# Attention layers: seven batches in one block with counting semaphores, a deferred MLP residual, and constant rows filled by DMA

## The reference

```python
h = _modulate(_layernorm(x), shift_msa, scale_msa)
x = x + gate_msa * _attention(h, ...)            # softmax(q k^T / sqrt(d)) v, projected
h = _modulate(_layernorm(x), shift_mlp, scale_mlp)
x = x + gate_mlp * (gelu(h @ W1 + b1) @ W2 + b2)
```

## Time and profile before

| | us |
|---|---|
| median of 3 runs | 6445.23 |
| the profiled execution | 6451.02 |
| its span | 6449.2 |
| setup, to the start of layer 0's first batch | 91.6 |
| layer 0, eight batches | 915 |
| layer 1, eight batches | 1567 |
| layer 2, eight batches | 986 |
| layer 3, eight batches | 2890 |

### The profile page before, as it was taken

How to read it: one execution, slowest core, us unless ns; L and a number is a source line. 1 busy time by engine, 2 the same in 40 slices (tenths; PEclk the granted TensorE clock), 3 DMA queues, 4 the chain that set the end, 5 groups by cost and what they waited for, 6 DMA issues and landing times. The chain is left out here.

```text
span 6449.2 us, 77669 instructions
## 1 busy us (share of the span) xinstructions
PE 5852.0 (91%) x28624; PEld 3040.1 (47%) x28624; DVE 4487.7 (70%) x4943; ACT 4214.9 (65%) x6876; POOL 2663.0 (41%) x1964
## 2 busy tenths in 40 slices
PE   8899899999999998998998888988898888888887
PEld 4444444555554554444444444444444444444444
DVE  5665654334444345666565998989898998989897
ACT  2354445444455443443434998989898998989896
POOL 0000002222222222000000886959596886959596
PEclk8999999999999999999999999999999999999999
DMA  4313220000000002222131202010101102011100
GB/s 114 60 30 54 36 50 22 1 1 1 1 1 1 1 1 48 40 48 47 32 59 23 59 21 55 29 49 29 47 30 35 41 22 55 29 47 30 47 29 19
DMA packets 152665, 216.11 MB, mean 34 GB/s; under 512 B 24224, under 2 KB 91064, under 8 KB 152032
## 3 DMA queue, kind: packets, MB, share of 16 engines
q1 hardware_dynamic: 152288, 211.14, 14.3%
HBM read 146.54 MB, written 30.44 MB: 27 GB/s over the span
## 5 line engine op out<-in xcount | busy, mean ns | idle before, releaser
L2230 DVE TENSOR_TENSOR_SCAN l__h<-l__decay,psum 128x1024 f32<-128x1024 f32 x1024 | 2276.5, 2272 | 79.1 <-ACT l__decay L1826 28.4
L2214 POOL TENSOR_TENSOR l__hc<-l__h,l__c_rep 128x1024 f32<-128x1024 f32 x1024 | 2039.0, 2004 | 189.2 <-DVE l__h L2230 126.6
L1826 ACT ACTIVATE l__decay<-l__dt_rep,l__a_neg 128x511 f32<-128x511 f32 x2048 | 1485.5, 845 | 14.9 <-DVE l__h L2230 14.8
L1833 PEld LDWEIGHTS psum<-ident,l__dtx_B 128*128 128x128 f32 x8192 | 892.2, 142 | 1108.8 <-DVE l__h L2230 683.1
L1833 PE MATMUL psum<-ident,l__dtx_B 128*128 128x128 f32 x8192 | 1132.0, 282 | 264.0 <-ACT l__dtx_B L1811 186.9
L1811 ACT ACTIVATE l__dtx_B<-l__dtx_T,l__b_T 128x512 f32<-128x512 f32 x1792 | 1328.4, 839 | 37.8 <-PEq L2325 35.8
L2299 PE MATMUL psum<-l__hc,l__gather 128*64 128x512 f32 x4096 | 1116.6, 624 | 10.2 <-POOL l__hc L2214 9.7
L193 POOL TENSOR_SCALAR l__ln_var_eps<-l__ln_mean_var 128x4 f32<-128x4 f32 x64 | 17.9, 279 | 2103.3 <-DVE l__ln_mean_var L179 2102.7
L675 DVE TENSOR_REDUCE l__row_max<-psum 128x1 f32<-128x512 f32 x1024 | 659.1, 687 | 267.1 <-PE psum L690 265.4
L1335 POOL TENSOR_SCALAR l__probs<-l__probs,l__rec 128x512 f32<-128x512 f32 x512 | 351.1, 699 | 966.7 <-DVE l__rec L1331 966.6
L1007 ACT ACTIVATE l__probs<-psum 128x1024 f32<-128x1024 f32 x512 | 516.4, 1026 | 285.4 <-PE psum L1068 278.6
(11 more groups left out here) (165 smaller groups left out, 7069.8 us busy)
## 6 DMA issues: line engine op xcount, KB each, us to landing
l__c_rep<-l__c_dram SPq DMA_DIRECT2D x512, 128.0 KB, 2.8
l__dt_rep<-l__dt SPq DMA_DIRECT2D x128, 256.0 KB, 5.1
l__parts_dram<-l__parts SPq DMA_DIRECT2D x64, 384.0 KB, 3.6
l__q_stack<-l__parts_dram SPq DMA_DIRECT2D x192, 128.0 KB, 6.4
l__k_stack<-l__parts_dram SPq DMA_DIRECT2D x192, 128.0 KB, 8.8
l__w<-in_l_w SPq DMA_DIRECT2D x6, 1024.0 KB, 7.6
in_mod_w<-in_mod_w SPq DMA_DIRECT2D x1, 4608.0 KB, 16.4
out_x<-x_sb SPq DMA_DIRECT2D x8, 512.0 KB, 3.2
```

What stands on the lines that cost most here:

```text
L1826: nc.scalar.activation(decay[:, i % DECAYS, s, 1:T], dt_rep[:, w, c, s, 1:T], ACT.Exp, scale=a_neg[:, g, c, s:s + 1]).then_inc(S["decay"], 1)
L1833: last = nc.tensor.transpose(bx_psum(i)[:, s, t * P:(t + 1) * P], dtx_B[:, (k + 1) % 2, t, 2 * c + s, :, :].rearrange("p j d -> p (j d)"), ...
L2214: nc.gpsimd.tensor_tensor(hc[:, i % HCS, :, :], h[:, i % HS, :, :], c_of_i, ALU.mult).then_inc(S["hc"], 1)
L2230: nc.vector.tensor_tensor_scan(both(h[:, i % HS, :, :]), both(decay[:, i % DECAYS, :, :]), both(bx_psum(i)), 0.0, ALU.mult, ALU.add).then_ ...
```

## The change

- `Semaphores` gets a count for each batch (`each`) and `at(name, n)`, which gives the semaphore and `batch * each + n`; all waits go through it.
- In the narrow and the wide layers the engines' programs are functions of a batch (`sync_batch`, `gpsimd_batch`, `vector_batch`, `scalar_batch`, `tensor_batch`). Batches 0 to 6 are one block without barriers between them, batch 7 is a second block. Layer 3 keeps a block for each batch.
- Waits that were only implied by the barrier are written out: the first late scores on the early maxima, `scores_T(0)` on the first max rows, `values(0)` and the first max transposes on the residual, in the wide layer the first scores, transposes and projection on what the batch before still held.
- Narrow layers, batches 0 to 5: the MLP residual is done in the next batch, after its third late tile (`RESIDUAL_AT = LEAD + 2`); the `cur` copy and the gates' products move there too. The other batches keep it at their end.
- Narrow layers: the first max rows of the next batch are made after early tile 20 (`FIRST_ROWS_AT = GT + 4`) and not after tile 23.
- The constant rows of the key stack come by DMA from a row of ones in DRAM (`ones16`, written in the setup), no `memset`; `first_gpsimd` does not wait for `rstd` any more.
- Setup: `second_tensor` follows the 14th of the `REST` fills.

```diff
+    def at(self, name, n):
+        return self.of[name], self.batch * self.each.get(name, 0) + n
...
         def first_sync(sp):
             valid_sync(sp, 0)
-            qkv_sync(sp, 0, True)
+            for row in range(k_max, k_all):
+                sp.dma_start(ks[row:row + 1, :, :],
+                             io["ones16"].unsqueeze(1).broadcast_to([1, H, T])).then_inc(S["ones_in"], 16)
+            qkv_sync(sp, 0)
+            sp.wait_ge(*S.at("ones_in", 16 * (k_all - k_max)))
             max_rows_in(sp, 0, 1)
 
         def first_gpsimd(pool):
-            pool.wait_ge(S["rstd"], 1)
-            nc.gpsimd.memset(ks[STACK:k_all, :, :], 1.0).then_inc(S["ones"], 1)
-            pool.wait_ge(S["ones"], 1)
             nc.gpsimd.memset(va[:, :, :, HD:2 * HD], 1.0).then_inc(S["ones"], 1)
...
-                    second_tensor(pe)
                     rest = iter(setup.REST)
-                    for _ in range(len(setup.REST) - LEAD // 3):
+                    for n in range(len(setup.REST) - LEAD // 3):
                         setup.fill(pe, next(rest))
+                        if n == SECOND_AT:
+                            second_tensor(pe)
...
+            for n in range(LEAD, TILES + GT):
+                if n < TILES:
+                    take_max(dve, n, n - LEAD + 1)
+                if n == RESIDUAL_AT:
+                    if S.batch:
+                        S.batch -= 1
+                        mlp_residual(dve, x[:, b - 1, :, :])
+                        S.batch += 1
+                    nc.vector.tensor_copy(cur[:, :], mod[:, b, mod0:mod0 + n_mod]).then_inc(S["cur"], 1)
+                    if gated:
+                        dve.wait_ge(*S.at("cur", 1))
+                        gates.vector(nc, dve)
...
+                for n in range(LEAD):
+                    take_max(dve, n, LATER + n + 1)
+                    if n == FIRST_ROWS_AT:
+                        make_max_rows(dve, bank[EARLY_MAX_BANK], NG)
+            if b + 1 >= JOINED:
+                mlp_residual(dve, x_b)
...
+                        early_scores(pe, early, LATER)
+                        if early == FIRST_ROWS_AT:
+                            pe.wait_ge(*S.at("max_taken", LATER + GT))
+                            max_transposes(pe, 0, bank[EARLY_MAX_BANK])
+                        early += 1
...
         def body(following):
-            for b in range(B):
-                more, more2 = b + 1 < B, b + 2 < B
-                F = None if more else following
+            for part in (range(JOINED), range(JOINED, B)):
+                F = following if part.stop == B else None
                 with nc.Block() as block:
...
                     @block.tensor
                     def _(pe):
+                        for b in part:
+                            S.batch = b - part.start
+                            tensor_batch(pe, b, F)
...
                 m = 3 * pair + t
                 if t < 3 and m < IN_LOOP:
                     if m:
                         pe.wait_ge(*S.at("proj", m))
+                    elif S.batch:
+                        pe.wait_ge(*S.at("res", 1 - RES_STEPS))
                     project(pair_of(m), t, bank[PROJ_BANK])
```

More of the change, by code:

```diff
@@ L465, in mask_rows @@
     def mask_rows(self, dve):
+        self.nc.vector.memset(self.ones16[:, :], 1.0).then_inc(self.s_mask, 1)
         dve.wait_ge(self.s_mask_in, 16)
@@ L874, in alone, with about, mlp_residual, sync_batch @@
             nc.all_engine_barrier(sems_to_clear=S.range)
+        def about(b):
+            return b + 1 < B, b + 2 < B, x[:, b, :, :]
+        def mlp_residual(dve, x_b):
+            residual(nc, dve, S, bank[6:8], b2[:, :], gates.rows[:, 1, :] if gated else None, tmp, x_b, 1,
+                     "down_filled")
+        def sync_batch(sp, b, F):
+            more, more2, x_b = about(b)
+            if b == 0:
+                late_sync(sp)
+            if F:
+                F.load(sp)
+            if more:
+                valid_sync(sp, b + 1)
+            for gg in range(1, NG):
+                max_rows_in(sp, gg, gg)
+            if more:
+                qkv_sync(sp, b + 1)
+                max_rows_in(sp, 0, NG)
+            if F:
+                sp.wait_ge(*S.at("oT", NG))
+                F.sync(sp)
@@ new lines, in gpsimd_batch @@
+        def gpsimd_batch(pool, b, F):
+            more, more2, x_b = about(b)
+            if b == 0:
+                late_gpsimd(pool)
+            if F:
+                F.gpsimd_begin(pool)
+                F.rstd(pool)
+                pool.wait_ge(*S.at("oT", NG))
+                F.gpsimd_heads(pool)
+            norm.gpsimd(nc, pool, 0)
+            if more2:
+                norm.gpsimd(nc, pool, 1)
+            if F:
+                F.gpsimd(pool)
+                F.gpsimd_second(pool)
@@ L986, in _ @@
-                        if more2:
-                            ahead.vector(nc, dve, b + 2, 1)
-                        if more:
-                            for n in range(LEAD):
-                                take_max(dve, n, LATER + n + 1)
-                            make_max_rows(dve, bank[EARLY_MAX_BANK], NG)
-                        residual(nc, dve, S, bank[6:8], b2[:, :], gates.rows[:, 1, :] if gated else None, tmp, x_b, 1,
-                                 "down_filled")
-                        if F:
-                            F.vector_end(dve)
+                        for b in part:
+                            S.batch = b - part.start
+                            vector_batch(dve, b, F)
@@ new lines, in gpsimd_batch @@
+        def gpsimd_batch(pool, b, F):
+            more, n_mlp, x_b = about(b)
+            for i in range(EARLY):
+                if i == SCALED_AT - 1 and more:
+                    norm.gpsimd(nc, pool, 0)
+                if i == NEXT_SCALED_AT - 1 and F:
+                    F.rstd(pool)
+                pool.wait_ge(*S.at("rec", i + 1))
+                normalise(i + LEAD)
+            norm.gpsimd(nc, pool, n_mlp)
+            if more:
+                for i in range(EARLY, UNITS):
+                    pool.wait_ge(*S.at("rec", i + 1))
+                    normalise(i - EARLY)
+            if F:
+                pool.wait_ge(*S.at("oT", PAIRS))
+                pool.wait_ge(*S.at("rstd", n_mlp + 1))
+                F.gpsimd(pool)
+                F.gpsimd_second(pool)
@@ L1390, in body @@
+        def body(following):
+            for part in (range(JOINED), range(JOINED, B)):
+                F = following if part.stop == B else None
                 with nc.Block() as block:
@@ L1468, in _ @@
-                        if more:
-                            for i in range(EARLY, UNITS):
-                                maxima(i)
-                            for i in range(EARLY, UNITS):
-                                sums_inverted(i)
-                        residual(nc, dve, S, bank[6:8], b2[:, :], gates.rows[:, 1, :], tmp, x_b, 1, "down_filled")
+                        for b in part:
+                            S.batch = b - part.start
+                            vector_batch(dve, b, F)
```

1439 lines of the change are left out of this document (725 added, 714 removed).

## The result

| | before | after |
|---|---|---|
| median of four runs each, one chip, us | 6447.47 | 6409.89 (6409.23 to 6412.81) |
| ratio, 95% interval | | 0.9942 (0.993 to 0.9954) |
| span of the profiled execution, us | 6449.2 | 6408.5 |

The account below looks back on a forecast made before the run. TensorE, busy 91%, was taken as the bound, with idle time at barriers and holds. Layer 1 28.6, layer 0 13, layer 2 9, setup 9 and hand-over 7.5 sum to 67 us: 6445.2 to 6378 us, range 6348 to 6404.

Parts of the forecast that it names:

- Layer 1, 28.6 us: Wide layer, six barriers gone: TensorE's 3.44 us gaps close, 20.6 us, and cold clock starts vanish, 8 us.
- the hand-over, 7.5 us: Layer 1 to layer 2: without GpSimd's memset holding VectorE 6.4 us gained, plus 1.1 us less at 1.2 GHz.
- Setup, 9 us: Setup: earlier norm without the memset and fills put before the second transposes gain 9 us, bounds 5 and 10.
- The parts 2.6 and 6.4: Setup: norm 2.6 us earlier without the memset; TensorE's 6.75 us wait filled by 14 fills, less 0.4 us.
- the fills take the same in either clock (they are 8 columns wide): Setup: TensorE's fills were assumed to take 0.85 us each whatever the granted clock.
- Layers 0 and 2, 22 us: Narrow layers, six barriers gone each and residual deferred: 13 us in layer 0 and 9 us in layer 2.
- The count of VectorE's chain: Narrow-layer boundary, tiles 24 to 30: layer 0 has 10.9 us, 8.1 of it work; gain 2.5 us, layer 2 2.1.
- less 0.3 us since in such a pause the clock can fall too: Layer 0 boundary: clock allowance taken off the 2.5 us gain, leaving 2.2 us, six times.
- the 0.6 us of layer 2: Layer 2 boundary: allowance for the clock falling in the residual's pause, taken off 2.1 us, leaving 1.5 us.
- the residual eats the narrow layers' gain: Rival, chance 0.17: in the narrow layers' tile loop the residual makes TensorE idle and cool; 45 us saved, 6400 us.
- The other three: Rivals: whole pause absorbed (0.12, 6325 us); GpSimd's hold stays (0.06, 6387); late tiles stay at 1.2 GHz (0.03, 6571).
- narrow batches not shorter: Sign of being wrong: batches of layers 0 and 2 fail to shorten, against a forecast 1.5 to 2.5 us.

Follow-up runs that it names:

- experiment 7: The kernel after, with the key stack's ones written by GpSimd's memset again instead of by DMA: 6413.05 us, ratio 0.9962 to the kernel before.
- experiment 1: The kernel after, but narrow layers have a block and barrier per batch again, residual at its end, old tile order: 6395.23 us, ratio 0.9938 to the kernel before.
- experiment 12: The kernel after itself, unchanged, run again beside the other follow-ups: 6397.81 us, ratio 0.9945 to the kernel before.
- experiment 3: The kernel after without the MLP residual of batches 0 to 5 in both narrow layers (output incomplete): 6338.02 us, ratio 0.9848 to the kernel before.
- experiment 4: The kernel after, with ScalarE copying the MLP's banks to SBUF, VectorE adding the residual after the last tile's maximum, gates' copy later: 6322.47 us, ratio 0.9823.
- experiment 2: The kernel after, with the joined narrow batches' residual at the end of its own batch instead of after tile 26: 6399.22 us, ratio 0.9941.

## Why the prediction was wrong

- *Layer 1, 28.6 us, and the hand-over, 7.5 us*: right. The batches are 187.7 us as forecast, layer and hand-over together give 36.1 (29.4 and 6.7), and experiment 7 brings the hold back at 6.7 us.
- *Setup, 9 us*: 15.0 measured. The parts 2.6 and 6.4 are right (2.7 and 6.7). Wrong is "the fills take the same in either clock (they are 8 columns wide)": 0.45 us a fill at 2.4 GHz, 0.85 at 1.2, and eleven of the 28 run at 2.4 GHz now. 4.5 us. The last 1.1 us are not accounted for.
- *Layers 0 and 2, 22 us*: this is the step that failed. Measured against the old form with nearly the same start (experiment 1), the joined and deferred form gives -0.4 us in layer 0 and +3.5 in layer 2 (-0.9 and -2.0 by experiment 12). The count of VectorE's chain was right up to tile 30 (2.2 and 1.4 us a batch). What failed is the price of the clock, "less 0.3 us since in such a pause the clock can fall too" and the 0.6 us of layer 2. I priced it only as a difference at the boundary. In truth every boundary kept a stretch at 1.2 GHz. In layer 0 it was 6.8 us before and is 3.4 to 10.2 now; in layer 2 it even shrank from 10.2 to 6.8 us, but begins 23 us after tile 0 instead of 18 to 20. As the tiles come earlier and the stretch stays or comes later, it lies over tiles 30 to 40, which cost 1.4 and 0.9 us more a batch. Within one kernel, experiment 3, these ten tiles take 8.14 us without a stretch there and 9.6 or 9.7 with one.
- *The tail* was not in the sum, beyond "where in a batch the clock falls shifts with every start, which moves the sum by a few us". Layer 2 differs by 9 us between two profiles of the same code, and from batch to batch by 3.2 us. With the 22 us lost and the setup's 6 gained the time would still be near 6396 us, inside the range (an estimate, 6447.5 less 15.0 and 36.1); the 8.8 us of layer 2's old code and the 3.5 of the new one take it out. The edges themselves do not follow from the words beside them, which give 6352 and 6407 us and not 6348 and 6404; the time lies outside these too.
- *Rivals*: "the residual eats the narrow layers' gain" (6400 us, given 0.17) had the right size. Its mechanism is partly right: experiments 3 and 4 show that the pause costs more than the residual's time. But experiment 2 shows the same cost with the residual at its old place. That the residual need not be in the loop or ahead of it at all (experiment 4, 75 us) I did not consider. The other three did not come: the pause was not absorbed, the hold by GpSimd is gone (8.36 to 1.69 us), and the loop does not stay at 1.2 GHz to its end.
- *What was to show it*: The batches of layer 1 are alike at 187.7 us. A sign of being wrong came too, "narrow batches not shorter": batches 1 to 6 take a mean of 114.6 us in layer 0 (114.4 before) and 119.4 in layer 2 (118.4 before). Layer 0's first `cur` came at 79.5 us, not at 82 to 83. "VectorE never idle between tile 24 and tile 30" is false (0.31 us ahead of tile 26 and 0.59 ahead of tile 30 above); the rows' DMA cost 0.2 to 0.3 us as said.

Open is why a stretch takes 3.4 us in one batch and 6.8 or 13.7 in the next of the same code, and whether layer 2's 9 us come from its start, the chip or the single execution. No run here controlled where the stretches begin.

## What to carry to other kernels

A barrier or pause taken out of a loop that is tight for TensorE pays only if the granted clock stays up: compare idle and busy time of the same matmuls before and after, since a gain in idle time can come back as busy time. Look for bunches of very narrow matmuls behind a short wait, which the busy share shows as full, and spread them between wide ones: here that was worth 44 us, a third of it beside the clock, where the barriers of both narrow layers gave nothing. Elementwise work that only needs a PSUM bank freed can be split: an idle engine copies the bank out, and the work follows where its engine waits (75 us here).

## What the hardware showed that I had not expected

- Twelve more 512-column matmuls a batch made the kernel 9 us faster: the clock stayed at 2.4 GHz across 24 four-column ones.
- The clock fell in the tail with no gap of TensorE over 0.56 us in the rows before, and in the setup in the midst of 56 eight-column matmuls with no gap at all. The Trainium skill ("TensorE: Matmul & The Clock Gate", section "HAM oscillation — how this bites in real kernels") finds the cause of such falls in long waits for a DMA. At the boundary there is a long wait here too, though for VectorE (5.49 and 6.94 us before); in the tail and in the setup there is none.
- The same code of layer 2 took 953 and 962 us (old form) and 960 to 966 us (joined) in different executions, with the granted clock as the difference to be seen: 123 us of it at 1.2 GHz in the first, 147 in the second.
- A fill of four 8-column fp32 matmuls takes 0.45 us at 2.4 GHz and 0.85 us at 1.2, 1.9 times as long: matmuls of eight columns slow down with the clock no less than the 512-column value matmuls above (1.06 to 1.94 us, 1.8 times).
